# A graph attention layer on one core: the start of the program put in another order, and edge keys spread by transfers instead of matmuls

## The reference

```python
h = jnp.maximum(_layernorm(x, axis=-1), 0.0)
q = h @ wq.T + bq; k = h @ wk.T + bk; v = h @ wv.T + bv
q2 = (q @ wiq.T + biq)...; k2 = (k @ wik.T + bik)...; v2 = (v @ wiv.T + biv)...   # 16 heads x 384 x 64
mask = full((384, 384), -inf); mask[src, dst] = softplus(edge_type_weights)[edge_type - 1]   # 6528 edges
# an edge of the diagonal that none of these sets has softplus(weights)[3]
attn = softmax(q2 @ k2.T / 8 + mask)
out = x + (attn @ v2) @ wo.T + bo
```

## Time and profile before

| | |
|---|---|
| median of 3 runs | 318.69 us (318.6 to 318.95) |
| the profiled execution | 318.79 us |
| its span, first to last instruction | 317.3 us |
| PE busy | 299.7 us, 94% |
| DVE / ACT / POOL busy | 179.1 / 154.7 / 147.0 us |
| first real PE work (transposes) | 13.91 us |
| first matmul of tile 1, of tile 2 | 24.22 us, 28.70 us |

### The profile page before, as it was taken

How to read it: one execution, slowest core, us unless ns; L and a number is a source line. 1 busy time by engine, 2 the same in 40 slices (tenths; PEclk the granted TensorE clock), 3 DMA queues, 4 the chain that set the end, 5 groups by cost and what they waited for, 6 DMA issues and landing times.

```text
span 317.3 us, 4822 instructions
## 1 busy us (share of the span) xinstructions
PE 299.7 (94%) x1744; PEld 270.1 (85%) x1744; DVE 179.1 (56%) x476; ACT 154.7 (49%) x288; POOL 147.0 (46%) x152
## 2 busy tenths in 40 slices
PE   1779999999999999999999999999999998899995
PEld 0469999888899999999998988898989896687894
DVE  4889867854354444444477656565656555543215
ACT  3664532334343333333335576767676677762210
POOL 5332755455354555440002964656565656954000
PEclk9999999999999999999999999999999999999999
DMA  7925533445944333466423231212122222300005
GB/s 205 361 68 201 169 112 118 135 135 178 349 134 135 115 118 113 127 199 211 132 78 122 66 135 67 64 71 68 66 67 68 66 67 69 132 2 0 0 2 198
DMA packets 13639, 37.47 MB, mean 118 GB/s; under 512 B 3248, under 2 KB 4528, under 8 KB 13616
## 3 DMA queue, kind: packets, MB, share of 16 engines
q1 hardware_dynamic: 11312, 35.93, 34.4%
q0 software_dynamic: 2016, 1.21, 1.5%
q10 hardware_dynamic: 288, 0.03, 0.1%
HBM read 34.38 MB, written 2.78 MB: 117 GB/s over the span
## 4 chain that ended last, share of the span: by engine, by line
PE 79%; DVE 9%; ACT 5%; issue 3%; DMA 2%; SPq 1%; POOL 0%; DVEq 0%; ACTq 0%
PE bank L767 23%; PE bank L763 22%; PE bank L764 22%; PE bank L893 4%; PE bank L880 3%; DMA x_sb<-in_x 2%; PE bank L908 2%; ACT prob L461 2%; PE bank L909 2%; DVE work L704 1%; DVE pt_lo L695 1%; ACT work L475 1%; DVE prob L681 1%; DVE x_sb L755 1%; ACT k_hi L395 1%
## 5 line engine op out<-in xcount | busy, mean ns | idle before, releaser
L352 POOL DMA_INDIRECT cells<-value,cell x51 | 56.2, 1102 | 57.7 <-DMA cells<-value,cell 44.8
L763 PE MATMUL bank<-a_hi,w_hi 128*128 128x384 f32 x192 | 65.3, 340 | 0.9 <-DVE w_lo L630 0.9
L767 PE MATMUL bank<-a_lo,w_hi 128*128 128x384 f32 x192 | 64.5, 336 | 1.1 <-DVE a_lo L643 1.0
L390 ACT ACTIVATE w_hi<-raw 128x1024 fp32r<-128x1024 f32 x51 | 53.5, 1054 | 21.9 <-PE bank L767 18.4
L764 PE MATMUL bank<-a_hi,w_lo 128*128 128x384 f32 x192 | 64.2, 334 | 0.0
L630 DVE TENSOR_TENSOR w_lo<-raw,w_hi 128x1024 fp32r<-128x1024 f32 x37 | 45.3, 1225 | 18.3 <-ACT w_hi L390 16.2
L369 POOL TENSOR_SCALAR prob<-prob,row_inv 128x384 f32<-128x384 f32 x36 | 22.6, 637 | 69.5 <-DVE row_inv L691 69.5
L767 PEld LDWEIGHTS bank<-a_lo,w_hi 128*128 128x128 f32 x192 | 36.0, 188 | 1.8 <-DVE a_lo L643 1.7
L763 PEld LDWEIGHTS bank<-a_hi,w_hi 128*128 128x128 f32 x192 | 36.1, 188 | 1.4 <-DVE w_lo L630 1.1
L764 PEld LDWEIGHTS bank<-a_hi,w_lo 128*128 128x128 f32 x192 | 36.1, 188 | 0.0
L695 DVE TENSOR_TENSOR pt_lo<-bank,pt_hi 128x384 fp32r<-128x384 f32 x48 | 25.2, 552 | 17.0 <-ACT pt_hi L468 17.0
(11 more groups left out here) (135 smaller groups left out, 618.9 us busy)
## 6 DMA issues: line engine op xcount, KB each, us to landing
raw<-in_slabs SPq DMA_DIRECT2D x56, 512.0 KB
x_sb<-in_x SPq DMA_DIRECT2D x5, 512.0 KB, 6.0
out_y<-x_sb SPq DMA_DIRECT2D x5, 256.0 KB, 2.2
cells<-prob SPq DMA_DIRECT2D x2, 576.0 KB, 9.5
cells<-value,cell POOLq DMA_INDIRECT x51
work<-cells POOLq DMA_DIRECT2D x1, 576.0 KB, 5.1
prob<-cells POOLq DMA_DIRECT2D x1, 576.0 KB, 7.1
x_sb<-in_x SPq DMA_DIRECT2D x2, 256.0 KB, 3.5
```

What stands on the lines that cost most here:

```text
L352: nc.gpsimd.indirect_dma_start(out=cells[c][:, :], out_offset=bass.IndirectOffsetOnAxis(ap=cell[:, t:t + 1], axis=0), in_=value[:, t:t + 1 ...
L390: nc.scalar.activation(split_place(s)[0], raw[:, s % RAW, :], ACT.Copy).then_inc(slab_hi, 1)
L763: nc.tensor.matmul(psum, w[0], a[0], start=first, stop=False)
L767: return nc.tensor.matmul(psum, w[0], a[1], start=False, stop=last)
```

## The change

The changed program does the following.

- SP asks for x first, in six halves of a node tile, then slab 0, then the edges (three transfers), then slabs 1 and 2 and the two fills of the cells.
- PE turns x by node tile: for node tile 0, 1 and 2 in turn, seven blocks of columns are turned into seven banks, with warm-up matmuls between (8 before, then 3, 3 and 2). The eighth block, whose bank is the first one's, is turned behind the first three matmuls of tile 0. Then all of tile 0 follows.
- DVE no longer handles edges before x. `edge_keys` and `edge_values` stand behind the eight `a_lo`, and unit 0 behind `split_lo(2)`.
- POOL makes the low part of slab 1 (before, DVE did). ACT splits slab 1 behind the fifth `a_hi` instead of behind the eighth. POOL's first half of slab 0 now also waits for `h_last_ok`, the last half tile of x from DVE.
- The keys are no longer spread by PE. DVE makes a row of keys (`key_row`, 51 x 128), SP writes it to DRAM, waits for it, and reads it back 13 times, each time 512 keys to all 128 partitions (256 KB), into parts of `work2`, `work` and `prob` that are free by then. DVE's comparison reads these copies in SBUF instead of a PSUM bank. `select` and its two steps on POOL are gone.

The diff, cut to its core:

```diff
-WARM = 13
+WARM = [8, 3, 3, 2]
-        key_bank = bank[0:2]
-        h_bank = [bank[5], bank[4], bank[7]]
+        h_bank = [bank[5], bank[4], bank[7], bank[6], bank[0], bank[1], bank[2], bank[5]]
         def lo_by_vector(s):
-            return 1 <= s < LO_ALL
+            return 2 <= s < LO_ALL
@@ SP
+            def load_keys(pos):
+                unit = UNIT_ORDER[pos]
+                part = key_rows[0:1, unit * EG * P:(unit * EG + len(tiles_of(unit))) * P]
+                sp_eng.dma_start(key_copy(pos), part.to_broadcast([P, len(tiles_of(unit)) * P])).then_inc(
+                    keys_in[pos], 16)
+                if s == 3:
+                    sp_eng.wait_ge(key_row_ok, 1)
+                    sp_eng.dma_start(key_rows[0, :].rearrange("(t e) -> t e", e=P), key_row[:]).then_inc(keys_out, 16)
+                    sp_eng.wait_ge(keys_out, 16)
+                    for pos in range(2):
+                        load_keys(pos)
@@ POOL
+            pool.wait_ge(h_last_ok, 1)
             for b in range(2):
                 half = slice(b * HALF, (b + 1) * HALF)
...
+            split_lo(1)
             done = 0
@@ ACT
-                if k == 0:
+                if k == 1:
                     first_slab_hi(1)
-            for s in range(1, AHEAD):
+                if k == 4:
+                    split_hi(1)
+            for s in range(2, AHEAD):
                 split_hi(s)
@@ DVE
-                if k == 3:
-                    edge_values()
-            edge_unit_cells(0)
-            for s in range(1, AHEAD):
+            edge_keys()
+            edge_values()
+            for s in range(2, AHEAD):
                 split_lo(s)
+            edge_unit(0)
             for s in range(QK0 + TILES_AHEAD):
@@ PE
-            for k in range(KT):
-                if k == HALF // P:
-                    pe.wait_ge(h_last_ok, 1)
-                if k >= 3:
-                    pe.wait_ge(h_lo, k - 2)
-                for t in range(NT):
-                    mm = nc.tensor.transpose(h_bank[k % 3][:, t * P:(t + 1) * P], x_sb[:, t, k * P:(k + 1) * P], ident[:])
-                mm.then_inc(h_turned, 1)
-                if k >= 2:
-                    tile(0, a_hi, a_lo, [k - 2])
+            for t in range(NT):
+                pe.wait_ge(h_ok, t + 1)
+                for k in range(KT - 1):
+                    if t == NT - 1 and k == HALF // P:
+                        pe.wait_ge(h_last_ok, 1)
+                    turn_h(k, t)
+                warm(WARM[t + 1])
+            for k in range(KT):
+                tile(0, a_hi, a_lo, [k])
+                if k == 0:
+                    for t in range(NT):
+                        turn_h(KT - 1, t)
             for t in range(KT):
                 if t >= 1:
                     tile(t, a_hi, a_lo)
-                keys(t + 2)
             for s in range(VV0, Q0):
-                if s + 2 < GROUPS:
-                    keys(s + 2)
-                if s == VV0 + KS:
-                    pe.wait_ge(later_ok, ET)
```

More of the change, by code:

```diff
@@ L103, in gat_kernel @@
         cols = sb("cols", [P, 2, ET], F32)
-        rows_i = sb("rows_i", [P, P], I32)
-        rows = sb("rows", [P, P], F16)
+        rows_i = sb("rows_i", [ET, 2, P], I32)
+        rows = sb("rows", [ET, 2, P], F32)
+        key_row = sb("key_row", [ET, P], F32)
         key = sb("key", [P, ET], F32)
@@ L270, in _ @@
                 sp_eng.dma_start(raw[:, s % RAW, :], slabs[s]).then_inc(slab_in[s % RAW], 16)
-                if s == 1:
+                if s == 0:
+                    sp_eng.dma_start(cols_i[:], edge_cols).then_inc(edges_in, 16)
+                    for i in range(2):
+                        sp_eng.dma_start(rows_i[:, i, :], edge_rows[i * DST_ROW:i * DST_ROW + ET, :]).then_inc(edges_in, 16)
+                if s == 2:
                     for c in range(2):
@@ L767, in products @@
                 return nc.tensor.matmul(psum, w[0], a[1], start=False, stop=last)
-            def keys(pos):
-                tiles = tiles_of(UNIT_ORDER[pos])
-                if pos >= 2:
-                    pe.wait_ge(later_ok, (pos - 1) * EG)
-                for i, t in enumerate(tiles):
-                    mm = nc.tensor.matmul(key_bank[pos % 2][:, i * P:(i + 1) * P],
-                                          select[:, t:t + 1].to_broadcast([P, P]), rows[:], start=True, stop=True)
-                mm.then_inc(keys_done, 1)
             def split_slab(s):
@@ L816, in moving, with warm, turn_h @@
                         mm.then_inc(done, 1)
[L818 to L823 removed]
+            def warm(n):
+                for _ in range(n):
+                    nc.tensor.matmul(tile_bank[0][:, 0:N], above[:], iota[:], start=True, stop=True)
+            def turn_h(k, t):
+                mm = nc.tensor.transpose(h_bank[k][:, t * P:(t + 1) * P], x_sb[:, t, k * P:(k + 1) * P], ident[:])
+                if t == NT - 1:
+                    mm.then_inc(h_turned, 1)
+            pe.wait_ge(x_in[0][0], 16)
             pe.wait_ge(iota_ok, 1)
[L825 to L828 removed]
+            pe.wait_ge(above_ok, 1)
+            warm(WARM[0])
             pe.wait_ge(ident_ok, 1)
[L830 to L841 removed]
+            for t in range(NT):
[5 more added lines that the diff above has]
+                warm(WARM[t + 1])
+            for k in range(KT):
+                tile(0, a_hi, a_lo, [k])
+                if k == 0:
+                    for t in range(NT):
+                        turn_h(KT - 1, t)
             for t in range(KT):
```

110 lines of the change are left out of this document (51 added, 59 removed).

## The result

The changed kernel takes **320.42 us** (median of 7 runs, 319.45 to 320.82) against 318.69 before (also 7 runs, 318.6 to 318.95): 1.0047 times as long, with a 95% interval of 1.0037 to 1.0056. It was forecast at 317.9, a little faster; it is a little slower, by more than the 0.2% that a measurement can tell. The profiled execution took 320.54 us, 1.75 more than that of before, with a span of 318.8 us.

What follows compares the result with a forecast made beforehand. PE was taken as the bound, the end moving with the start of tile 2 and PE's work behind it: 318.79 - 0.3 - 2.1 = 316.4, plus 1.5 for the clock, 317.9 us; range 315.2 to 320.0, leaving out 2 in 10.

Steps and rivals of the forecast that it cites:

- The likeliest case: PE idle 5.7 us between tiles 1 and 2, waiting for DVE; clock falls, 317.0 to 318.9, chance 0.40.
- keys later than forecast and a clock at its full price and more: Unit 0 on DVE waits for late keys: 320.0 with clock up, 321.5 down; chance 0.17, shared with the full clock price.
- T, the third transpose: At the start, third transpose of the first block of columns done, ACT can begin `a_hi`: 12.4 us, from 11.5 to 13.0.
- DVE is free by then: At the start, DVE is free when x's first half lands at 3.0 to 4.3; first statistics taken at 3.8.
- From T to tile 1: Tile 1 starts at T + 6.0 = 18.4, after POOL's low part of slab 1; 5.8 us earlier than before.
- From T to tile 2: DVE's edge steps, wait for keys, units 0 and 1, slab 3 and `b_lo` end at T + 16.0.
- The clock: PE's clock falls in the gap ahead of tile 2, costing between nothing and 2.3 us; 1.5 taken.
- The keys off PE: Behind the start of tile 2, 35 matmuls of 128 columns at 0.06 us leave PE: 2.1 us less.
- X: Start of tile 2 on PE: 12.4 + 16.0 = 28.4, only 0.3 us ahead of 28.70 before.
- The chance for slower (0.17): For the whole kernel, the chance of a time more than 0.2% (0.6 us) above before: 0.17.
- the better start: Clock comes up during the transposes, casts aren't held: T = 11.5, X = 26.8, time 314.8; chance 0.12.

Runs made afterwards that it cites:

- the version of 311.5 us: Changed kernel with edge values behind `tile_lo_part(0)`, units 0 and 1 behind `tile_lo_part(1)`, later units behind each tile's low part, key row written behind slab 4: 311.5 us.

## Why the prediction was wrong, point by point

The likeliest case was the right one: a long gap ahead of tile 2, made by DVE, in which the clock falls. The order of events is as forecast down to the cast that waits for POOL. But that case was held to end by 318.9; keys later than forecast and a clock at its full price and more, the case that I gave 0.17, is what the trace shows on top of it. The sum was 2.6 us short, in three terms, against one that was too small the other way.

- **T, the third transpose: 13.4 instead of 12.4.** The first half of x landed at 4.17, not 3.8, and DVE then first did its small steps on the edge weights, for which it waits until 4.31, so that the first statistics stand at 4.70. The step "DVE is free by then" failed on a transfer that I hadn't looked for. The third `shift` was at 11.08 instead of 9.8, and PE's first transposes stood at 8.94 instead of 7.7, 1.2 us late. From there to T it took 4.4 us, 0.3 less than the 4.7 forecast: the transposes, 1.73 and 1.33 us per node tile, were at the slow end of the range of 0.8 to 1.5 and beyond, but the 4.7 had room for it. So the +1.0 us comes from the late first statistics, not from slow transposes, as I still had it when I expected the run with 18 warm-up matmuls.
- **From T to tile 1: 6.0, as forecast** (13.38 to 19.39).
- **From T to tile 2: 17.1 instead of 16.0.** DVE reaches the comparison at T + 10.5 (10.7 forecast). The keys come at T + 12.0 instead of T + 11.3. The write was shorter than its bound (1.64 for 2.2), the load far longer (3.75 for 2.4). The mis-sized term is the load, which I priced by the **stored** outputs, though loads of the same size stood in the same group with 3.5 us at least. I set those aside because the queue looked empty; the run with the load alone shows that an empty queue gives 3.2. Nor was it an idle queue on which the stores took 2.2, as the prediction says: all seven were issued within 4 us (310.92 to 314.90). The two units took 3.22 instead of 2.96, and 0.15 passes from `b_lo` to PE. +1.1 us. The comparison of keys in SBUF costs what it did in PSUM, 0.27 from one to the next.
- **The clock: 2.6 instead of 1.5.** That it falls was right, by the trace and by the fill of the gap. I took a price between nothing and 2.3, without a row for the lower end, while the row of the start (4.6 us at the low level) spoke for 2.3. In all twelve executions of the three kernels with a gap of 4.5 us or more the clock fell (means of 0.983 to 0.989), and 5.6 us of matmuls ran at half speed in the profiled one of the changed kernel. +1.1 us. The price isn't one number, though: 2.6 and 2.7 us behind gaps of 6.7 and 4.5, 1.7 behind 8.4 and about 1.5 behind 2.0. What sets it these runs don't show. The Trainium skill's warning that long idle gaps between bursts of matmuls put the clock back (TensorE: Matmul & The Clock Gate, Why this matters for your kernels) holds here at 4.5, 6.7 and 8.4 us; it fell behind 2.0 us too, and at 1.75 and 1.82, in one trace each, it didn't.
- **The keys off PE: 2.6 instead of 2.1.** A group of four cost 0.30 us in the tile's period, not the 0.20 read from the starts around it. The rest stands behind the group: the first product is then 0.26 us ahead of the next (28.70 in the earlier trace rows to the line below), and 0.17 where tile follows tile without a group (24.07 to 24.24 in the version of 311.5 us). -0.5 us.

```profile
28.96 0.34 PE L764 MATMUL bank<-a_hi,w_lo 128*128 128x384 f32 x1
```

In all +1.0 + 1.1 + 1.1 - 0.5 = 2.7, and 320.54 - 317.9 = 2.6. Before the measurement X = 28.4 lay only 0.3 us ahead of the old 28.70, so that a slip of 1 us in the start or in the keys was enough to turn the sign. The chance for slower (0.17) was too small for that: start, keys and clock were each held at a good value. Each of these errors alone makes about 318.9 of 317.9, within 0.2% of before, and any two of them about 320.0, beyond it. One rival was also added up wrongly: the better start is said to have "the clock as above", but its 314.8 leaves the 1.5 us of the clock out; with them it is 316.3.

As to the parts by themselves, measured where no gap hides them: x first is worth 1.4 to 2.0 us, keys off PE 2.2 to 2.7, slab 1 on POOL 0.56 as a wait of PE and 0 to 0.5 in the times, within their spread. The change as made spends all of it, and 1.75 us more, at one place on DVE.

## What to carry to other kernels

When work is put ahead of the step that frees a buffer for the bound engine, count that engine's gap, and if the engine is PE count the clock too: here a gap of 6.7 us came with 2.6 us of clock on top, and moving the same work behind the freeing step (`tile_lo_part`) turned 0.5% slower into 2.1 to 2.3% faster. Move such work no further back than its own chain allows: scatters that started at 37 us instead of 28 were too late for a step of DVE at 154. And price a load by a load of its size, not by a store: here stores of 256 KB took 2.1 to 2.3 us and loads 3.2 to 3.8.

## What the runs showed of the hardware that was not expected

- The price of a fall of the clock didn't follow the length of the gap. Behind 6.7 us of idle PE the clock was down from about 26 to 36.1 and 5.6 us of matmuls ran at half speed; behind 4.5 us, from 29.3 to 36.1 and 5.8 us; behind 8.4 us, from 29.0 to 35.8 and 3.8 us. Behind 2.0 us, at 161 to 163 in the version with all edge steps behind, it was down for 3.4 us.
- At the start the level can be lost again while transposes run. In the profiled execution of the version of 311.5 us PE is idle for 2.35 us ahead of 9.01 and for 0.33 ahead of 10.79; the granted clock goes to 0.50 at about 10.8 and back at about 14.2, and seven transposes take 1.75 instead of 0.95 us. With the edges ahead of x the idle times are 1.29 and 1.54 us, and the clock is down from about 12.1 to 15.5. With 18 warm-up matmuls from 2.46 on it isn't lost, though 1.81 us and 0.34 us of idle time stand in the same places.
- The granted clock of the profile doesn't show the level at which a program begins. It reads full through the start of both kernels, where warm-up matmuls of 384 columns are 0.33 us apart. Later falls it does show, as 0.50, those above at the start and the one ahead of tile 2.
- Loading 256 KB into SBUF took 3.2 us alone and 3.4 for x's first half, storing them 2.1 to 2.3. A slab of 512 KB alone took 3.3.
- An int32 cast of 51 x 256 on DVE takes 0.81 us if it begins beside POOL's low part and 0.28 otherwise.
